# The mask of a two-stream local attention moved from VectorE's score pass into a bf16 identity product on TensorE

## The reference

```
sim  = (8 * q/|q|) . (k/|k|)         # 128 queries x 256 keys: window before and own window
mask = (i < j) | (i > j + 128) | (j == -1)
sim  = where(mask, -max, sim);  attn = softmax(sim);  out = attn @ v
x = x + out @ wo;  x = x + gated MLP(layernorm(shift(x)))
```

## Time and profile before

| what | value |
|---|---|
| time, median of 3 runs | 5743.0 us (5729.33 to 5743.41) |
| profiled execution | 5745.5 us, of which the span is 5743.6 us |
| busy share of the span: PE, PEld, DVE, ACT, POOL | 92%, 54%, 74%, 47%, 18% |
| second stage | from about 2300 us to the end |

### The profile page before, as it was taken

How to read it: one execution, slowest core, us unless ns; L and a number is a source line. 1 busy time by engine, 2 the same in 40 slices (tenths; PEclk the granted TensorE clock), 3 DMA queues, 4 the chain that set the end, 5 groups by cost and what they waited for, 6 DMA issues and landing times.

```text
span 5743.6 us, 93748 instructions
## 1 busy us (share of the span) xinstructions
PE 5265.5 (92%) x29772; PEld 3081.9 (54%) x29772; DVE 4255.0 (74%) x11183; ACT 2725.2 (47%) x5409; POOL 1022.7 (18%) x1341
## 2 busy tenths in 40 slices
PE   4989898989898988899999999999999999999998
PEld 1232323232323232577777777776777776777776
DVE  5878686878687876677777777777777777777776
ACT  0535353535353545444444444454454454444544
POOL 1010100101010100222222222222222222222221
PEclk7989898999898999999999999999999999999999
DMA  4332322232323130000000000000000000000000
GB/s 106 94 60 34 60 34 60 33 60 33 60 34 67 35 62 16 33 7 9 8 7 26 13 7 9 8 7 26 12 7 10 6 7 27 11 6 10 6 8 6
DMA packets 163936, 161.02 MB, mean 28 GB/s; under 512 B 26100, under 2 KB 155976, under 8 KB 163408
## 3 DMA queue, kind: packets, MB, share of 16 engines
q1 hardware_dynamic: 163536, 156.42, 13.1%
HBM read 111.48 MB, written 44.09 MB: 27 GB/s over the span
## 4 chain that ended last, share of the span: by engine, by line
PE 68%; DVE 19%; issue 6%; DMA 2%; SPq 2%; POOL 1%; ACT 1%; DVEq 0%; POOLq 0%; ACTq 0%
PE psum L811 13%; PE psum L743 9%; PE psum L613 8%; DVE mx L1071 8%; PE psum L583 7%; PE psum L718 6%; PE psum L782 4%; PE psum L791 4%; PE psum L603 4%; PE psum L774 3%; PE psum L766 3%; PE psum L755 2%; DVE big_s L1267 2%; PE psum L552 2%; DMA stack<-parts_d 1%
## 5 line engine op out<-in xcount | busy, mean ns | idle before, releaser
L1071 DVE TENSOR_REDUCE mx<-psum 128x1 f32<-128x512 f32 x2048 | 1323.2, 686 | 338.9 <-PE psum L583 334.6
L865 ACT ACTIVATE pr<-psum 128x1024 f32<-128x1024 f32 x1024 | 1000.2, 1021 | 1061.3 <-PE psum L603 1061.2
L583 PE MATMUL psum<-stack 96*128 96x512 bf16 x2048 | 833.7, 413 | 187.4 <-DVE mx L1071 89.7
L906 ACT ACTIVATE big_s<-big_s,mxl_s 128x256 f32<-128x256 f32 x1024 | 507.5, 496 | 656.1 <-DVE mxl_s L1275 656.1
L811 PE MATMUL psum<-hlT_s,w_sb 128*128 128x128 f32 (+1 forms) x6144 | 786.9, 281 | 24.3 <-DVE hlT_s L1312 21.9
L811 PEld LDWEIGHTS psum<-hlT_s,w_sb 128*128 128x128 f32 (+1 forms) x6144 | 693.0, 180 | 158.2 <-ACT hlT_s L921 55.3
L743 PE MATMUL psum<-wqkv_sb,uT_s 128*128 128x512 f32 x1536 | 748.7, 610 | 1.0 <-DVE uT_s L1228 1.0
L583 PEld LDWEIGHTS psum<-stack 96*128 96x128 bf16 x2048 | 198.8, 97 | 979.4 <-DVE mx L1071 866.4
L603 PE MATMUL psum<-stack 99*128 99x512 bf16 x2048 | 628.3, 390 | 19.8 <-issue 18.3
L613 PE MATMUL psum<-pr,vg 128*32 128x512 f32 x4096 | 549.4, 610 | 0.4 <-ACT pr L865 0.4
L766 PE MATMUL psum<-kT_s,qz_s 128*128 128x256 f32 x2048 | 517.9, 391 | 0.0
(11 more groups left out here) (166 smaller groups left out, 6534.4 us busy)
## 6 DMA issues: line engine op xcount, KB each, us to landing
stack<-parts_d SPq DMA_DIRECT2D x384, 128.0 KB, 6.4
parts_d<-parts SPq DMA_DIRECT2D x64, 384.0 KB, 2.5
hn<-in_x SPq DMA_DIRECT2D x8, 1024.0 KB, 9.2
xr<-in_x SPq DMA_DIRECT2D x8, 1024.0 KB, 5.7
x_d<-xr SPq DMA_DIRECT2D x8, 1024.0 KB, 4.4
tab<-tab_d SPq DMA_DIRECT2D x32, 256.0 KB, 2.6
mask_s<-in_mask SPq DMA_DIRECT2D x64, 128.0 KB, 2.3
out_x<-o_s SPq DMA_DIRECT2D x64, 128.0 KB, 1.7
```

The source lines that it names most:

```text
L583: pe.matmul(psum[:, 6 + kh, :], stack[0:KS, g % 2, 0, u % 2, h, a * P:(a + 1) * P], stack[0:KS, g % 2, 1, kh, h, :], start=True, stop=True ...
L865: act.activation(pr[:, e % 2, 2 * pair:2 * pair + 2, :], psum[:, 2 * pair:2 * pair + 2, :], ACT.Exp, scale=DH ** -0.5).then_inc(s_exp, 1)
L906: ins = act.activation(w["big"][:, h, :], w["big"][:, h, :], ACT.Exp, bias=w["mx"][:, h:h + 1], accum_out=w["z"][:, h:h + 1])
L1071: dve.tensor_reduce(mx[:, u % 2, m, kh:kh + 1], psum[:, 6 + kh, :], AX.X, ALU.max).then_inc(s_max, 1)
```

## The change

PE first writes the mask into the whole bank (two heads) with one bf16 product: the identity stands, and the mask tile, now bf16 and read twice, moves through. The two score products of the bank then accumulate on it. DVE no longer makes a scaled and masked copy: B2 and B2b are gone, B2a and B2c take the maxima of four heads from two PSUM banks in one `tensor_reduce`, and one small instruction forms `nb = -mx * rn`. ACT's exponentials read PSUM, with `rn` as scale and `nb` as bias, and write `big`. B2a now waits for `s0` and `s1` before it begins, B2c for `s2` and `s3`. The score banks are held until the exponentials are done.

The masks take a new way. Both kinds of tile (window 0, and all others) are loaded once before the second stage's other inputs, DVE turns them into bf16 (`maskb`), and SP copies one to a stream's tile for each window, from SBUF to SBUF, as soon as the stream's last scores of the window before are done. PE waits for it in `s0`.

```diff
@@ SP
                 if wait:
-                    sp.wait_ge(w["s_sm"], it * 8)
+                    sp.wait_ge(w["s_s_ps"], it * 8)
                     sp.nop(nofuse=True)
-                sp.dma_start(w["mask"][:], mask[bass.ds(t, 1)].rearrange("o p n -> p (o n)")).then_inc(w["s_mask_in"], 16)
+                sp.dma_start(w["mask"][:], maskb[:, 0 if is_window(t, 0) else 1]).then_inc(w["s_mask_in"], 16)
...
+            sp.dma_start(maskf[:], mask[0:2].rearrange("t p n -> p t n")).then_inc(s_maskf_in, 16)
             pair_in(0, False)
             pair_in(0, True)
+            sp.wait_ge(s_maskb, 1)
+            sp.nop(nofuse=True)
             window(0, 0, 0, prev=False)
@@ PE
                     if name == "s0":
                         pe.wait_ge(w["s_qz"], n + 1)
                         pe.wait_ge(w["s_kT"], n + 1)
+                        pe.wait_ge(w["s_mask_in"], it * 16 + 16)
                     if name == "s2":
                         pe.wait_ge(w["s_vev"], n + 1)
+                    pe.matmul(psum[:, bk + int(name[1]), :], identb[:],
+                              w["mask"][:].unsqueeze(1).broadcast_to([P, 2, 2 * P]), start=True, stop=False)
                     for h in (2 * int(name[1]), 2 * int(name[1]) + 1):
                         mm = pe.matmul(psum[:, bk + h // 2, (h % 2) * 2 * P:(h % 2 + 1) * 2 * P], w["qz"][:, h, :],
-                                       w["kT"][:, l, h // 2, :], start=True, stop=True)
+                                       w["kT"][:, l, h // 2, :], start=False, stop=(h % 2 == 1))
@@ ACT
-                        ins = act.activation(w["big"][:, h, :], w["big"][:, h, :], ACT.Exp, bias=w["mx"][:, h:h + 1],
+                        ins = act.activation(w["big"][:, h, :], psum[:, bk + h // 2, (h % 2) * 2 * P:(h % 2 + 1) * 2 * P],
+                                             ACT.Exp, scale=w["rn"][:, h:h + 1], bias=w["nb"][:, h:h + 1],
                                              accum_out=w["z"][:, h:h + 1])
@@ DVE
-                elif name in ("B2", "B2a", "B2b", "B2c"):
-
-                    if name == "B2":
-                        dve.wait_ge(w["s_mask_in"], it * 16 + 16)
+                elif name in ("B2a", "B2c"):
+
+                    a = 0 if name == "B2a" else 4
+                    if a == 0:
                         dve.wait_ge(w["s_rn"], n * 4 + 4)
-                    for h in {"B2": range(0, 2), "B2a": range(2, 4), "B2b": range(4, 6), "B2c": range(6, 8)}[name]:
-                        if h % 2 == 0:
-                            dve.wait_ge(w["s_s_ps"], n * (LH // 2) + h // 2 + 1)
-                            dve.nop(nofuse=True)
-                        ins = dve.tensor_tensor_reduce(out=w["big"][:, h, :],
...
-                        dve.tensor_scalar(w["mx"][:, a:a + 4], w["mx"][:, a:a + 4], -1.0, None, ALU.mult).then_inc(w["s_sm"], 1)
+                    dve.wait_ge(w["s_s_ps"], n * (LH // 2) + a // 2 + 2)
+                    dve.tensor_reduce(w["mx"][:, a:a + 4], psum[:, bk + a // 2:bk + a // 2 + 2, :]
+                                      .rearrange("p b (h k) -> p (b h) k", k=2 * P), AX.X, ALU.max).then_inc(w["s_sm"], 1)
+                    dve.wait_ge(w["s_sm"], n * 4 + (a // 2 + 1))
+                    dve.scalar_tensor_tensor(out=w["nb"][:, a:a + 4], in0=w["mx"][:, a:a + 4], scalar=-1.0,
+                                             in1=w["rn"][:, a:a + 4], op0=ALU.mult, op1=ALU.mult).then_inc(w["s_sm"], 1)
...
+            dve.wait_ge(s_maskf_in, 16)
+            dve.tensor_copy(maskb[:], maskf[:]).then_inc(s_maskb, 1)
             dve.wait_ge(s_xs0_in, 64)
```

More of the change, by code:

```diff
@@ L154, in build @@
             zero = tmp("zero", [P, P])
+            maskf = tmp("maskf", [P, 2, 2 * P])
+            maskb = tmp("maskb", [P, 2, 2 * P], BF16)
             gateF = tmp("gateF", [P, 2, D])
@@ L158, in build @@
                 u=tmp(f"u_s{s}", [P, D]),
-                mask=tmp(f"mask_s{s}", [P, 2 * P]),
+                mask=tmp(f"mask_s{s}", [P, 2 * P], BF16),
+                nb=tmp(f"nb_s{s}", [P, LH]),
                 x1n=tmp(f"x1n_s{s}", [P, 6]),
@@ L241, in build @@
         s_zero = sem("s_zero")
+        s_maskf_in = sem("s_maskf_in")
+        s_maskb = sem("s_maskb")
         for s in range(2):
@@ L1336, in turn @@
                 if prev:
-                    blk("B2b", Y, *before)
                     blk("B2c", Y, *before)
@@ L1347, in turn @@
                     blk("C2", Y, *before)
-                blk("B2", X, l, t, it)
                 if prev:
@@ L1353, in turn @@
                     blk("D1", Y, *before)
-                blk("B2b", X, l, t, it)
                 blk("B2c", X, l, t, it)
@@ L1374, in turn @@
                 blk("D2", X, l, t, it)
-                blk("B2", Y, l, t, it)
                 blk("B2a", Y, l, t, it)
@@ L1399, in _ @@
             finish_layer(X, 1, last * 2 + 1)
-            for name in ("B2b", "B2c"):
-                blk(name, Y, 1, t, last)
+            blk("B2c", Y, 1, t, last)
             finish(X, 0, t, last)
```

## The result

The changed kernel takes **5767.1 us** (median of 5 runs, 5763.5 to 5775.3) against 5741.0 us (median of 5, 5729.3 to 5743.4): ratio 1.0051, 95% interval 1.0036 to 1.0066. It is slower by more than 0.3%, but by 26 us and not by the 72 of the forecast. The profiled execution took 5775.3 us, with a span of 5773.5 us.

What follows compares the result with a forecast made beforehand. PE was taken to pace Y's score steps and DVE X's score stretch; 40 + 8 + 22 + 2 = 72 us on the profiled 5745.5 us gave 5817.5, forecast as 5815 us against the 5743.0 median, range 5765 to 5865 us.

Steps and rivals of the forecast that it cites:

- X's term: Stream X's score stretch: B2a with four heads delays D1 and Yw1a by 0.35 us in 64 halves, 22 us.
- DVE's relief as idle time: DVE, second stage: masked passes replaced by reductions, about 100 us less busy, gained as idle time and not on the path.
- the hidden masks: SP's mask copy for each window: issued early enough that PE's new wait in s0 is met at all windows.
- PE's unbroken chain: Stream Y's score steps: in 46 halves PE runs from Ys0 into Xq01 without a gap, so added products are exposed.
- The start: Second stage's start: one mask load of 256 KB ahead of the inputs, 2 us with its issue.
- The 18 halves with a late F X: Stream Y, where PE waits for F X: B2c's small instruction 0.46 us late in each half, 8 us.
- The product in Y, 46 x 0.88 = 40 us: Stream Y's halves without a gap: four identity products of 0.22 us each fully exposed on PE, 40 us.
- The lower price: PE's identity product in Y at the skill page's 131 ns for a sustained stream: 24 us in place of 40.
- ACT's exponentials, "0.50 us, no change": Exponentials reading PSUM with a scale operand: 0.50 us each, no change; at the upper end 0.605 us, costing 28 us.
- PE has room: Rival, chance 0.12: the products fit on PE in whole, only 22 + 2 = 24 us remain, 5767 us.
- The product is dear: Rival, chance 0.12: each identity product costs PE 0.44 us, the float32 rate; 121 us in all, 5864 us.
- faster: Rival, chance 0.07: DVE sets the pace of Y's softmax and its relief comes through, 29 us gained, 5714 us.

Runs made afterwards that it cites:

- e2: The changed kernel without the identity products, its mask left out of the computation: 5732.6 us.
- e9: The kernel before with 84 idle semaphore increments on DVE at the second stage's start, behind its wait for the zeroed semaphores: 5728.5 us, ratio 0.9972.
- e1: The kernel before with the new masks and identity products added, DVE's masked passes and ACT's exponentials kept: 5763.4 us.
- e8: The changed kernel with exponentials lacking the scale operand, the query's norm left out: 5765.0 us.
- e4: The kernel before with 84 idle semaphore increments on DVE, once, ahead of the loops: ratio 0.9967 to the kernel before.
- e13: The changed kernel with 98 idle semaphore increments on DVE ahead of the loops: 5789.8 us, ratio 1.0078 to the kernel before.
- e12: The changed kernel with 100 idle semaphore increments on DVE ahead of the loops: 5802.7 us, ratio 1.0096 to the kernel before.
- e14: The changed kernel with 102 idle semaphore increments on DVE ahead of the loops: 5774.0 us.

## Why the prediction was right or wrong

**What held.** X's term: B2a between C3 and D1 was put at 0.35 us a half. The way from X's kT transposes to Yw1a went from 7.10 us (4296.07 to 4303.17) to 7.44 (4311.16 to 4318.60), and e2 shows it alone. The reduction (1.22 us forecast, 1219 ns measured), DVE's relief as idle time, the hidden masks (no wait of PE in 64 halves) and PE's unbroken chain held as well. The start was put at 2 us, and 3.0 were seen.

**The 18 halves with a late F X: the step that failed most.** The prediction took DVE's 3.02 us of "issue" for a fixed cost of the branch and forecast 0.46 + 0.35 = 0.81 us more in each. Three of the 18 wait for a new pair's input. The other 15 were the stall, and it vanished: they lost 14.5 us in all and did not gain 12. That is 27 of the 48 us by which the halves fell short (70 forecast, 22 measured). Against e9, which is the kernel before without the stall, the 15 halves grew from 790.5 to 802.5 us, 0.80 each. That this meets the forecast 0.81 does not bear out its two terms: alone, the products cost such a half 0.39 us (e1's last pair) and the rest 0.19 (e2), and the 0.2 us left were not traced. In whole, the change costs 3368.5 - 3317.2 = 51 us of work against e9, and gets 29 us back in its halves by ridding DVE of the stall: 22 us, with the start and the end 26.

**The product in Y, 46 x 0.88 = 40 us: mis-sized.** A product does take its 0.22 to 0.23 us from start to start, as the rows of the first stage said (the chain has 0.21 to 0.32), but what stands behind it gets shorter. From start to start the four float32 passes behind another kind of work took 0.97 us before (1.06 in the chain), and 0.86 with a bf16 product ahead. That gives back 0.11 us twice, and `w2` and `q01` are 0.07 and 0.11 us shorter. So the chain from `s0` to the end of `q01` grew by 10.97 - 10.46 = 0.51 us and not 0.88, and `p` and the product with v behind it gave back some 0.1 more in e1, which has 0.39 for the half. The step that failed was to add the price of an instruction and leave its neighbours as they were. Why they get shorter is not shown. The lower price that the prediction set beside it, from the Trainium skill ("TensorE: Matmul & The Clock Gate", Back-to-back issue gap), was 131 ns; 0.51 / 4 = 0.13 us is the same figure as a net price, although from start to start no product took less than 0.21.

**ACT's exponentials, "0.50 us, no change": mis-sized.** They take 0.564 us. I had let the gain of reading PSUM and the scale operand cancel, and the operand costs 92 ns against 24 gained. From the start of `Yp` to that of the product with v it is 2.02 us, and 1.84 in e8. In an ordinary half the runs add up: 0.39 (the products, e1) + 0.27 (all but the products, e2) + 0.23 (the scale operand on top of both, e8) = 0.89 us, the measured 52.77 - 51.88, where the forecast had 0.88 + 0.35 = 1.23. Together the two mis-sized terms left the 43 halves that never stalled (the table's 38 and the last pair's 5) 17 us below the forecast. The last 4 of the 48 us lie around the changes of pair.

**The rivals.** "PE has room" gave 5767 us, the measured time to the microsecond, and that is luck: the loss of the stall hid more than half of the work's price. It is wrong as a mechanism, for the products cost 0.4 us a half (e1), and the chain without a gap shows no room, though the share of weight loads (2483 / 3428 = 72%) had spoken for it. "The product is dear" and "faster" fell: no `s` step took more than 1.18 us with its product, and no ordinary half went below 51.9 us. With the stall still there the time would have been about 5767 + 29 = 5796 us (an estimate), which the forecast's own 5785 to 5845 us hold. A rival in which the "issue" at the branch goes away was missing, and the earlier trace rows pointed at it: 3 us of idle time that the profile puts down to nothing.

## What to carry to other kernels

A long "issue" ahead of an engine's first instruction in a loop's body may be the loading of its code: look for packets of the instruction queue inside the wait and in each pass of the loop, and move the loop by some dozens of idle instructions before pricing anything, for here that alone was worth 0.3% with no work changed. Where two versions differ in code size, compare each at a place where it does not stall; the changed kernel's real price was 51 us, not 26. An added matmul is priced as the change of its whole group, its neighbours included. Costs found one at a time need not add up: the products alone and the rest alone gave 0.66 us a half, both together 0.89.

## What the runs showed that was not expected

- A semaphore increment costs DVE some 0.1 us: 84 of them made a half 8.8 us longer in e4.
- The same loop body, moved by 84 instructions, saves DVE 3 us of idle time at each of 15 branches, about 1.8 us of each half: 54.2 to 55.3 against 52.7 us.
- DVE's queue loads the loop's code anew in each pass, some five packets of 8192 bytes, or not at all, by the place of the code. The packet that a stall waits for lands 1.4 to 1.7 us before DVE goes on.
- Two instructions of shift (e13 to e12) change what the stall costs in the last pair from about 2 to 5 us a half, as the loop's first work then waits for two packets and not for one; two more (e14) take it away.
- A scale operand from SBUF makes a 128 x 256 exponential 92 ns longer (564 against 472), and its source in PSUM 24 ns shorter (496 to 472).
- Four float32 passes of 256 columns behind another kind of work took 0.97 us from start to start (1.06 in the chain), and 0.86 once a bf16 product of 512 columns stood ahead of them. The product's weight load took 97 ns, a float32 one 192.
